# Perceiver block, one core: second-batch expert tiles split in place in a ring of six, first-batch attention output and router in score banks, split expert bias, fused norms

## The reference, cut to what matters

```python
x = x + xattn(_layernorm(x), ctx, ctx)          # 16 heads of 32
x = x + attn(_layernorm(x))                     # ends in its own norm, times gamma plus beta
x = x + ffn(_layernorm(x))

def ffn(x):                                     # per token
    expert_idx = argmax(x @ W_router)           # 4 experts
    h = gelu(einsum('th,ehi->tei', x, W1) + b1) # W1: 4 x 512 x 2048
    intermediate = einsum('te,tei->ti', one_hot(expert_idx, 4), h)
    y = intermediate @ Wo + bo + x
    return layer_norm(y) * ln_gamma + ln_beta
```

## Time and profile before

| | |
|---|---|
| time of the three runs, median | 566.1 us |
| the profiled execution's own time | 568.86 us |
| span of its trace | 566.8 us |
| mean granted TensorE clock | 0.975 |
| TensorE matmul busy | 530.3 us, 94% |
| VectorE, ScalarE, GpSimd busy | 294.7, 209.1, 37.2 us |
| moved by DMA | 62.22 MB |

### The profile page before, as it was taken

How to read it: one execution, slowest core, us unless ns; L and a number is a source line. 1 busy time by engine, 2 the same in 40 slices (tenths; PEclk the granted TensorE clock), 3 DMA queues, 4 the chain that set the end, 5 groups by cost and what they waited for, 6 DMA issues and landing times.

```text
span 566.8 us, 8877 instructions
## 1 busy us (share of the span) xinstructions
PE 530.3 (94%) x3582; PEld 373.3 (66%) x3582; DVE 294.7 (52%) x608; ACT 209.1 (37%) x305; POOL 37.2 (7%) x32
## 2 busy tenths in 40 slices
PE   7999999999998989999997999798999999799895
PEld 6777776777776668987765777455765446566542
DVE  3635535747574642461964766612384427855332
ACT  3110026464645323273225364452163126544300
POOL 0210000000691000000000000000000000000000
PEclk8999999999998999999997999899999999999998
DMA  8700000000630003221000000942966677774000
GB/s 278 298 0 1 1 1 0 2 2 2 223 149 1 2 9 124 91 76 41 18 1 0 1 2 9 419 169 69 418 264 213 233 270 261 269 288 148 2 19 19
DMA packets 11311, 62.22 MB, mean 110 GB/s; under 512 B 1540, under 2 KB 2564, under 8 KB 4484
## 3 DMA queue, kind: packets, MB, share of 16 engines
q1 hardware_dynamic: 11272, 61.66, 29.2%
HBM read 61.13 MB, written 0.52 MB: 109 GB/s over the span
## 4 chain that ended last, share of the span: by engine, by line
PE 87%; DVE 6%; ACT 3%; issue 2%; DMA 1%; SPq 0%; POOLq 0%; POOL 0%; DVEq 0%; ACTq 0%
PE ps L942 40%; PE ps L1003 11%; PE ps L1192 10%; PE ps L989 6%; PE ps L1018 5%; PE ps L1233 4%; PE ps L1216 2%; DVE w1L L916 2%; PE ps L1218 2%; PE ps L1217 2%; DVE Pm L590 1%; ACT w1H L525 1%; DMA raw<-in_ctxT 1%; PE ps L1201 1%; PE ps L936 1%
## 5 line engine op out<-in xcount | busy, mean ns | idle before, releaser
L359 ACT COPY PT<-ps 128x512 f32<-128x512 f32 x96 | 53.4, 589 | 103.7 <-PE ps L1003 103.7
L1003 PE MATMUL ps<-ident,Pm 128*128 128x128 f32 x512 | 69.0, 277 | 1.6 <-ACT PT L359 0.7
L590 DVE TENSOR_SCALAR_CACHE_REDUCE Pm<-ps,small 128x512 f32<-128x512 f32 x96 | 66.4, 747 | 7.4 <-PE ps L989 7.2
L1003 PEld LDWEIGHTS ps<-ident,Pm 128*128 128x128 f32 x512 | 56.7, 141 | 19.6 <-issue 15.8
L351 ACT ACTIVATE Pm<-Pm,small 128x2048 f32<-128x2048 f32 x32 | 64.2, 2008 | 14.2 <-DVE Pm L590 14.2
L1192 PE MATMUL ps<-w1raw,z 128*128 128x512 f32 x128 | 60.2, 620 | 3.3 <-DVE Pm L590 3.3
L942 PE MATMUL ps<-ctxH,wkH 128*128 128x512 f32 x124 | 52.9, 427 | 5.9 <-DVE u L735 3.4
L942 PE MATMUL ps<-wvH,ctxH 128*128 128x512 f32 x128 | 51.6, 403 | 0.0
L942 PE MATMUL ps<-ctxL,wkH 128*128 128x512 f32 x124 | 50.3, 406 | 0.0
L942 PE MATMUL ps<-wvL,ctxH 128*128 128x512 f32 x128 | 50.1, 391 | 0.0
L942 PE MATMUL ps<-ctxH,wkL 128*128 128x512 f32 x124 | 50.1, 404 | 0.0
(11 more groups left out here) (165 smaller groups left out, 717.9 us busy)
## 6 DMA issues: line engine op xcount, KB each, us to landing
w1raw<-in_W SPq DMA_DIRECT2D x32, 1024.0 KB, 4.8
raw<-in_ctxT SPq DMA_DIRECT2D x7, 1024.0 KB, 4.8
woF<-in_ffn_Wo SPq DMA_DIRECT2D x4, 1024.0 KB, 15.8
raw<-in_ctxT SPq DMA_DIRECT2D x2, 512.0 KB, 6.1
wv_raw<-in_xWv SPq DMA_DIRECT2D x2, 512.0 KB, 8.4
wq<-in_xWq SPq DMA_DIRECT2D x1, 1024.0 KB, 13.0
wS<-in_xWo SPq DMA_DIRECT2D x1, 1024.0 KB, 7.0
wS<-in_wq SPq DMA_DIRECT2D x1, 1024.0 KB, 4.8
```

The costliest lines, as they stand in the source:

```text
L359: act.copy(PT[:, c % 2, i, :, :].rearrange("p k t -> p (k t)"), ps[:, T_BANKS[i % 2], :]).then_inc(pt_act, 1)
L590: dve.tensor_scalar(Pm[:, i, c * CH:(c + 1) * CH], ps[:, i, :], -1.0, mx[:, p % 2, i, c - 1:c] if c else NOT_YET, ALU.mult, ALU.min, accum ...
L1003: last = pe.transpose(ps[:, T_BANKS[i % 2], j * P:(j + 1) * P], Pm[:, i, c * CH + j * P:c * CH + (j + 1) * P], ident[:])
```

## The change

- Batch 1's expert tiles have a ring of their own of six (`w2raw`), in the places of `P2`/`PT2` of batch 1 and of the four old raw tiles. VectorE writes the low part over the raw tile (`w2L`, same addresses). The high part has three buffers. ScalarE copies tile n when tile n - 3 is finished; the transfer into a slot waits until TensorE has finished the tile in it. Tiles 0 and 1 are fetched during the first pass, after tiles 11 and 12.
- `attention2_out(0)` writes bank 0 and moves behind `keys(G + 2, 1)`; `normalized_T(0)` writes bank 0 and moves to pass G + 3, before `keys(G + 3, 1)`; the logits go to bank 1; `masks(0)` moves from chunk 3 to chunk 2 of pass G + 3. The wait for `u_done` moves from `keys(G + 2, 0)` to `scores(G + 2, 0)`. VectorE, no longer ScalarE, copies the transposed tokens of batch 0.
- VectorE computes the reciprocals of passes G - 1 and 7 during chunk 2 of the next pass; TensorE does `values(1, 0, 0)` before `reciprocals_T(G - 1)`.
- `first_experts(0)` waits bank by bank for the scores to be moved out.
- The bias `b1` is split into high and low (one copy of ScalarE, one subtraction of VectorE) and added by eight fp32r matmuls; for batch 1 this comes before tile 14, and gelu waits for the chunks of tile 15.
- `finish` and `normalized2` use two fused instructions, (t - mean) * gamma and t * rstd + residual, of which the first does not wait for the power.
- The hidden transposes of batch 0 follow tile 2, `ffn_out(0, 0..2)` follow tiles 6, 9 and 12.

```diff
...
 u = pair("u", [P, D], F32, 22, 182)
-ohT = pair("ohT", [E, P], F32, 22, 54)
+ohT = pair("ohT", [E, P], F32R, 22, 54)
 rows = at("rows", [P, 3, D], F32, 16)
...
 w1raw = [at(f"w1raw{i}", [P, I], F32, 64 + 8 * i) for i in range(RING)]
-w1H = [at(f"w1H{i}", [P, I], F32R, 128 + 16 * i) for i in range(2)]
-w1L = [at(f"w1L{i}", [P, I], F32R, 136 + 16 * i) for i in range(2)]
+RING2 = 6
+w2raw = [at(f"w2raw{i}", [P, I], F32, kb) for i, kb in enumerate((128, 136, 64, 72, 80, 88))]
+w2L = [at(f"w2L{i}", [P, I], F32R, kb) for i, kb in enumerate((128, 136, 64, 72, 80, 88))]
+w2H = [at(f"w2H{i}", [P, I], F32R, kb) for i, kb in enumerate((144, 152, 24))]
 b1raw = at("b1raw", [E, I], F32, 160)
+b1L = at("b1L", [E, I], F32R, 160)
+b1H = at("b1H", [E, I], F32R, 168)
 hid = pair("hid", [P, I], F32, 0, 168)
 hidT = pair("hidT", [P, IT, T], F32, 8, 56)
-uo = [at("uo_0", [P, D], F32, 24), u[1]]
+uo = u
...
 QKV_BANKS = [(0, 1, SPARE), (4, 5, SPARE)]
-O2_BANKS = (SPARE, 7)
-XT_BANKS = (SPARE, 4)
-LOGIT_BANKS = (0, 5)
+O2_BANKS = (0, 7)
+XT_BANKS = (0, 4)
+LOGIT_BANKS = (1, 5)
 MASK_BANKS = (SPARE, 6)
...
-        slot, r = n % RING, n - RING
-        if 0 <= r < NW1:
-            sp.wait_ge(first_tile, r + 1)
-        if r >= NW1:
-            sp.wait_ge(w1_split, r - NW1 + 1)
-        sp.dma_start(w1raw[slot][:], w1_v[n % NW1]).then_inc(w1_in[slot], 16)
+        if n >= RING:
+            sp.wait_ge(first_tile, n - RING + 1)
+        sp.dma_start(w1raw[n % RING][:], w1_v[n]).then_inc(w1_in[n % RING], 16)
+
+    def w2_tile_in(n):
+
+        if n < 2:
+            sp.wait_ge(pv2_mm, 2)
+        elif n < RING2:
+            sp.wait_ge(first_tile, NW1 - RING + n - 1)
+        else:
+            sp.wait_ge(w1_tile, n - RING2 + 1)
+        sp.dma_start(w2raw[n % RING2][:], w1_v[n]).then_inc(w2_in[n % RING2], 16)
...
         sp.dma_start(rowsF[:, n, :], a["rows"][4 + n:5 + n, :].to_broadcast([P, D])).then_inc(rowsF_in, 16)
-    for n in range(RING, 2 * NW1):
+    for n in range(RING, NW1):
         w1_tile_in(n)
+        if n in (11, 12):
+            w2_tile_in(n - 11)
         if RING <= n < RING + KT:
...
             sp.dma_start(woF[:, k, :], a["ffn_Wo"][:, k, :]).then_inc(woF_in, 16)
+    for n in range(2, NW1):
+        w2_tile_in(n)
     for b in range(B):
...
         for c in range(1, C):
-            if p == G + 2 and c == 3:
-                transposed(yT[0], x2T_mm, 0, XT_BANKS[0], x2T_done)
             if p == G + 3 and c == 3:
...
         if p == G:
+            while_values(0)
             reciprocals_T(p - 1)
-            while_values(0)
             exponentials(p, 0)
...
     values2(1)
+    act.wait_ge(b1_in, 16)
+    act.copy(b1H[:], b1raw[:]).then_inc(b1_hi, 1)
     act.wait_ge(cN_ready, 2)
...
     for n in range(NW1):
-        k = NW1 + n
-        act.wait_ge(w1_in[k % RING], 16 * (k // RING + 1))
-        if n == 1:
+        act.wait_ge(w2_in[n % RING2], 16 * (n // RING2 + 1))
+        if n == 0:
             act.wait_ge(cT_dve[1], 2 * HPG)
-        if n >= 2:
-            act.wait_ge(w1_tile, n - 1)
-        act.copy(w1H[n % 2][:], w1raw[k % RING][:]).then_inc(w1_hi, 1)
-        if n == 1:
+        elif n == 1:
+            act.wait_ge(o2_mm, 2)
+        elif n == 2:
+            act.wait_ge(first_tile, NW1)
+        else:
+            act.wait_ge(w1_tile, n - 2)
+        act.copy(w2H[n % 3][:], w2raw[n % RING2][:]).then_inc(w1_hi, 1)
+        if n == 2:
             gelu(0)
-        if n == 3:
+        if n == 4:
             hidden_T(0, 0)
...
+    def scaled(t, gamma, base_rows, n):
+
+        step(dve.scalar_tensor_tensor(t, t, meanvar[:, n, 0:1], gamma, ALU.subtract, ALU.mult))
+        dve.wait_ge(rstd_done, n + 1)
+        dve.scalar_tensor_tensor(base_rows, t, rstd[:, n:n + 1], base_rows, ALU.mult, ALU.add).then_inc(norm_done, 1)
+
     def normalized2(b):
-        normalize(u[b][:], u[b][:], LN3[b])
+        scaled(u[b][:], row["gamma"], xb[b], LN3[b])
         dve.wait_ge(norm_done, LN3[b] + 1)
-        step(dve.tensor_tensor(u[b][:], u[b][:], row["gamma"], ALU.mult))
-        step(dve.tensor_tensor(xb[b], xb[b], u[b][:], ALU.add))
...
         statistics(t, EPS_FFN, LN5[b])
-        normalize(t, t, LN5[b])
-        dve.wait_ge(norm_done, LN5[b] + 1)
-        step(dve.tensor_tensor(t, t, rowF["gamma"], ALU.mult))
-        dve.tensor_tensor(t, xb[b], t, ALU.add).then_inc(out_ready, 1)
+        step(dve.scalar_tensor_tensor(t, t, meanvar[:, LN5[b], 0:1], rowF["gamma"], ALU.subtract, ALU.mult))
+        dve.wait_ge(rstd_done, LN5[b] + 1)
+        dve.scalar_tensor_tensor(t, t, rstd[:, LN5[b]:LN5[b] + 1], xb[b], ALU.mult, ALU.add).then_inc(out_ready, 1)
...
             residual2(0)
-        if p == G + 1 and at_point == 3:
+        if p == G + 2 and at_point == "keys1":
             added_output2(0)
-        if p == G + 2 and at_point == "keys0":
             statistics(u[0][:], EPS, LN3[0])
-        if p == G + 2 and at_point == "keys1":
+        if p == G + 2 and at_point == 0:
             normalized2(0)
-        if p == G + 2 and at_point == 0:
+        if p == G + 2 and at_point == 1:
             statistics(xb[0], EPS, LN4[0])
-        if p == G + 2 and at_point == 1:
+        if p == G + 2 and at_point == 2:
             normalize(split4(xb[0]), y[0][:], LN4[0])
+        if p == G + 3 and at_point == "keys0":
+            dve.wait_ge(x2T_mm, 1)
+            dve.tensor_copy(yT[0][:], split4(ps[:, XT_BANKS[0], :])).then_inc(x2T_done, 1)
         if p == G + 3 and at_point == "keys1":
...
                     keys(p, 3)
+            if c == 2 and p in (G, NP):
+                reciprocals(p - 1)
             alongside(p, c)
         if p == G:
-            reciprocals(p - 1)
             outputs(p - 1)
...
             while_values(15)
-    reciprocals(NP - 1)
     outputs(NP - 1)
...
     values2(1, 1)
+    dve.wait_ge(b1_hi, 1)
+    dve.tensor_tensor(b1L[:], b1raw[:], b1H[:].bitcast(F32), ALU.subtract).then_inc(b1_lo, 1)
     denominators2(1)
...
         dve.wait_ge(w1_hi, n + 1)
-        if n == 1:
-            dve.wait_ge(o2_mm, 2)
-        if n >= 2:
-            dve.wait_ge(w1_tile, n - 1)
-        dve.tensor_tensor(w1L[n % 2][:], w1raw[(NW1 + n) % RING][:], w1H[n % 2][:].bitcast(F32),
+        dve.tensor_tensor(w2L[n % RING2][:], w2raw[n % RING2][:], w2H[n % 3][:].bitcast(F32),
                           ALU.subtract).then_inc(w1_split, 1)
...
             masked_both({1: 1, 2: 2, 4: 3}[n])
-        if n == 3:
+        if n == 4:
             hidden_T(0, 1)
             hidden_T(0, 3)
-        if n == 5:
+        if n == 6:
             ffn_residual(1)
...
             pe.wait_ge(cN_ready, 1)
+        if p == G + 2 and c == 0:
+            pe.wait_ge(u_done, 1)
         if p == G + 3 and c == 0:
...
         else:
-            pe.wait_ge(k_done, C * (G + 2))
+            pe.wait_ge(s_done, (G + 2) * C * HPG)
         product(ps[:, O2_BANKS[b], :], [(cT[b][:, k, :], wS[:, k, :]) for k in range(KT)]).then_inc(o2_mm, 1)
...
         if not b:
-            pe.wait_ge(k_done, C * (G + 3))
+            pe.wait_ge(s_done, (G + 3) * C * HPG)
         transposes([y[b][:, k, :] for k in range(KT)], XT_BANKS[b], x2T_mm)
...
-        if n == 0:
-            pe.wait_ge(s_done, NP * C * HPG)
         pe.wait_ge(z0_done, n // KT + 1)
...
         for c in range(IC):
+            if n == 0:
+                pe.wait_ge(s_done, (NP * C - 1) * HPG + c + 1)
             last = pe.matmul(ps[:, c, :], z[:, n, :], w1raw[n % RING][:, c * CH:(c + 1) * CH],
...
-        pe.wait_ge(b1_in, 16)
+        pe.wait_ge(b1_lo, 1)
         pe.wait_ge(ohT_ready, b + 1)
         for c in range(IC):
-            pe.matmul(ps[:, 4 * b + c, :], ohT[b][:], b1raw[:, c * CH:(c + 1) * CH], start=False, stop=True)\
-                .then_inc(w1_mm[b], 1)
+            for part in (b1H, b1L):
+                last = pe.matmul(ps[:, 4 * b + c, :], ohT[b][:], part[:, c * CH:(c + 1) * CH], start=False,
+                                 stop=(b == 0 and part is b1L))
+            if b == 0:
+                last.then_inc(w1_mm[b], 1)
...
         pe.wait_ge(w1_split, n + 1)
-        wH, wL = w1H[n % 2], w1L[n % 2]
+        wH, wL = w2H[n % 3], w2L[n % RING2]
         for c in range(IC):
...
             pe.matmul(dst, zH[:, n, :], wL[:, cc], start=False, stop=False)
-            last = pe.matmul(dst, zL[:, n, :], wH[:, cc], start=False, stop=False)
-        last.then_inc(w1_tile, 1)
+            last = pe.matmul(dst, zL[:, n, :], wH[:, cc], start=False, stop=(n == NW1 - 1))
+            if n == NW1 - 1:
+                last.then_inc(w1_mm[1], 1)
+        if n < NW1 - 1:
+            last.then_inc(w1_tile, 1)
...
         if more:
-            if p == G + 2:
-                pe.wait_ge(u_done, 1)
-            if p == G + 3:
-                pe.wait_ge(x2T_done, 1)
             keys(p, 0)
...
             reciprocals_T(p - 2)
+        if p == G + 3:
+            normalized_T(0)
         if more:
             keys(p, 1)
+        if p == G + 2:
```

(19 more changed lines are left out.)

2 lines of the change are left out of this document (added).

## The result

The changed kernel takes 547.46 us (median of four runs, 545.29 to 548.2) against 566.11 us (565.6 to 566.4) of the kernel before timed beside it: a ratio of 0.9665, with an interval from 0.9637 to 0.9693. A later series gave 547.89 against 566.83, 0.968 (0.9633 to 0.9728). In the first pair 18.65 us are won where 21.2 were predicted; the forecast of 544.9 is 2.6 too low, and its range (541.5 to 549.5) holds the time.

A forecast was written before the change was run, and what follows sets the result against it. TensorE was taken as the bound, 94% of the span busy. Terms 12.2 + 6.2 + 2.2 - 1.0 + 1.3 + 0.3 = 21.2 us, subtracted from the median 566.1, gave 544.9 us; range 541.5 to 549.5.

The forecast's parts named there:

- Second experts: From the end of first_experts(15) to ffn_out(0, 3): 75.7 us becomes 63.5, 12.2 us won, 3.6 of them bias.
- (b): Half of the 8.9 us of gaps in the second experts stays: 549.3 us; chance 0.11.
- (e): In the second experts, subtraction in place takes some 4.7 us a split and VectorE bounds the phase: 569.6 us; chance 0.03.
- (f): The experts' bias passes stay as slow, 3.6 us lost: 548.5 us; chance 0.03.
- Projection: `keys(G + 2, 0)` no longer waits for `u`; 3.46 us of wait and the half clock behind it go: 6.2 us won.
- (c): In pass G + 2, add and statistics before the third key move hold up the scores; clock falls: 548.7 us; chance 0.06.
- Masks: In chunk 2 of pass G + 3, `masks(0)` waits for VectorE to move the keys out: 1.0 us lost.
- Bank by bank: Before the first experts, the 3.3 us wait ends with `z0_done` and stays, half clock behind it: 0 won.
- (d): The clock holds at 362 us, behind the wait before the first experts: 3.1 us more won, 541.8 us; chance 0.05.
- Norm and tail: Fused norm wins 1.3 us in `finish(1)`, its first instruction beside the power, and 0.3 through `finish(0)`.
- (a): Fused instructions run at half speed, 1.23 us each; `finish(1)` wins 0.2 instead of 1.3: 546.0 us; chance 0.2.
- a low clock inside the second experts: Sign in the new trace: the forecast is wrong if the low clock shows up in the second experts; no size given.

The follow-up runs named there:

- the pair: Changed kernel with two high buffers instead of three in the second experts: 555.12 us, ratio 0.9785.
- the earlier `z`: Changed kernel with masks(0) two transposes later and expert 0's masked tokens computed before the last score moves: 541.17 us, ratio 0.956.
- the changed kernel again: The changed kernel, nothing altered, timed once more in a later series: 547.89 us, ratio 0.968.
- the reciprocals: Changed kernel with the reciprocals of passes 3 and 7 behind the chunks again and reciprocals_T(3) before batch 1's first values: 549.43 us, one run.
- the added 128-row run: Changed kernel with sixteen extra 128-row fp32r matmuls of 512 columns before tile 0 of the second experts: 549.41 us, ratio 0.9682.
- the bank: Changed kernel with batch 0's projection back in bank 6 at chunk 3 of pass G + 1: 552.5 us, ratio 0.9735.
- the masks: Changed kernel with masks(0) two transposes later in chunk 2 of pass G + 3: 544.9 us, ratio 0.9605.
- the three-instruction norm: Changed kernel with the last norm, in `finish`, in three VectorE instructions behind the power again, for both batches: 547.3 us, one run.
- the earlier `z` again: The kernel with expert 0's masked tokens computed earlier and masks(0) later, timed once more beside the spread bias: 542.75 us, ratio 0.9546.
- the bias spread: Kernel with the earlier `z`, its bias matmuls in pairs behind the chunks of a tile instead of one run per batch: 542.32 us, ratio 0.9559.

## Why the prediction was right, and what it missed

*Second experts: right.* 63.5 us predicted, 63.53 in the profiled run. The gaps are worth 8.3 by the pair (8.6 in the terms), the bias 3.2 by its records (3.6 predicted); the last 0.7 of the stage's 12.2 no run undoes. A run of eight takes 2.04 us, not 1.8, as the starts next to the change from and to 128 rows lie 0.1 further apart. That the length comes out to 0.03 us is luck in part: the bias was priced 0.4 too low, and the 0.3 left for rest was not needed. Rivals (b), (e) and (f) are out: no wait for a split, 2289 ns for each of them in place, eight records 0.23 apart.

*Projection: right.* 6.2 predicted, 6.36 between the traces, 5.4 when it alone is undone; the difference lies in how long the clock stays low, so the term is 5.4 to 6.4, and the prediction took the one trace that it had. Rival (c), a new wait in that pass, did not come: the 16.17 us window is all busy, at 1.00.

*Reciprocals: right*, 2.2 predicted, 2.2 between the traces and 2.2 when undone. *Masks: right*, -1.0 predicted, -1.1 in the trace, 0.9 of it given back when they move. *Bank by bank: right*, 0 predicted and the wait unchanged; the earlier `z` shows that VectorE's order was the reason. Rival (d), the clock holding there, did not come in the profiled run: 0.68 over the first tile instead of 0.55 is a fall that ended sooner. In the nine other profiles that keep this wait the clock fell there too. It held only where the wait was taken away.

*Norm and tail: right in kind, mis-sized.* 1.3 + 0.3 predicted, 1.2 measured. In `finish(1)` 0.8 us instead of 1.3: the fused instructions take 0.74 and 0.75 us instead of 0.69 (0.1), and the power beside the first of them 0.92 instead of 0.55 (0.4), which the prediction had put in parallel at no cost. Rival (a), 1.23 us each, is out. By that the trace contradicts the sentence of the Trainium skill (Vector Engine (DVE) Microarchitecture Reference, 7. Points that are easy to get wrong) on half throughput, for float32 sources. The slower power does agree with another of its rules: a VectorE instruction with two inputs in SBUF contends with a GpSimd instruction that reads SBUF (SBUF — State Buffer, Who interferes with whom).

*The sum.* The parts measured in the traces are 12.2 + 6.4 + 2.2 - 1.1 + 1.2 = 20.9 us, against 21.2 predicted; the medians differ by 18.65. What was off is not a term but the subtraction of the sum from the median, which takes the clock elsewhere as unchanged. The terms come from one long execution: its mean clock is 0.975, while 25 later ones of the kernel before had 0.972 to 0.990, eleven of them 0.984. It took 2.75 us more than its median, and the profiled run of the changed kernel 2.17 less than its own; that is the whole way from the 23.6 between the two profiled executions to the 18.65 between the medians. 2.5 of these 4.9 us are named above (start, first tile), and up to 1.0 may be the longer half clock behind the wait for `u`. The prediction named a low clock inside the second experts as a sign that it is wrong, and that sign came in some runs: in four of the nine profiled runs of kernels with this bias and this stage (the changed kernel again, the earlier `z`, the reciprocals, the added 128-row run) the clock fell right behind a bias, for 1.6 us each. In others (the changed kernel's first profile, the bank, the masks, the three-instruction norm, the earlier `z` again) it did not. Falls elsewhere vary as well. Here are the windows around the copy of `rexp` for which `reciprocals_T` waits in pass 4 (TensorE idles some 2 us), in the changed kernel:
```profile
166.00:180.00 14.00, 11.93 (x79) 9.18 (x78) 6.62 (x13) 9.12 (x11) 4.52 (x1) 0.88 0.00 0
```
and in the second run of the kernel with the earlier `z`:
```profile
166.00:180.00 14.00, 11.75 (x91) 8.87 (x89) 7.98 (x14) 9.75 (x12) 4.61 (x2) 1.00 0.00 0
```
The same wait, once with a fall and once without, is 1.3 us between the first scores and those of pass 4 (145.94 against 144.65). Such draws go with the spread within one kernel (5.1 us over the changed kernel's second four runs, the slower two at the lower clock). How they share out over the unprofiled runs of before and after, and so the missing 2.3 us, stays open: those runs show a mean clock only.

## What to carry to other kernels

When TensorE is the bound, cut both traces at the same instructions and compare stage by stage: a sum of removed waits, each with the slow clock behind it, then came out to some tenths here, while the medians still differed from it by some 2 us of the luck of the clock. Read the terms from more than one trace of before, since a low clock in one of them is counted as if it were always there. A wait for the first of four results is worth something only if that result is also made early; look at the order of the engine that makes it. Price an instruction that is to run beside one of another engine by a row in which both run, and long runs of matmuls like the bias by more than their own time. Of the versions here the one with the earlier `z` is the fastest: 541.17 and 542.75 us, 6.7 below the changed kernel in the series that has both; with the bias spread it is the same within the measurement.
